# Transposing the normalised tiles of the first stage by DMA: 24 of 32 tiles leave TensorE, the projections keep two PSUM banks

## Chip, cores and metric

One Trainium2 chip, 8 NeuronCores, each running the same program on its own inputs with no traffic between cores. The metric is device time in microseconds (us) of the slowest core, median of several runs.

## The reference

For each of 4 sequences of 4096 tokens with 1024 features, a pre-norm attention and a pre-norm feed-forward layer, cut to what matters:

```python
z = layernorm(x)                            # no gain, no bias
q, k, v = z @ Wq, z @ Wk, z @ Wv            # 64 columns each
att = softmax(einsum('bid,bkd->bik', q, k), axis=1)   # over the queries i
x = x + tile(att @ v, (1, 1, 16))
z = layernorm(x); z_prev = z shifted by one token
r = sigmoid((mu_r*z + (1-mu_r)*z_prev) @ W_r.T)
k = (mu_k*z + (1-mu_k)*z_prev) @ W_k.T
x = x + r * (square(relu(k)) @ W_v.T)
```

The softmax runs over the queries, so every key row needs its exponentials over all 4096 queries before its sum is known. A core owns 2048 query tokens of one sequence, but computes q, k and v of all 4096.

## The kernel before, in words

**First stage.** x comes in 32 tiles of 128 tokens (128 x 1024, float32) into a ring of 8 buffers, `xst`. VectorE takes the statistics of each tile (`stats`: two halves and an aggregate, L405 to L408). GpSimd makes the scale from them (L352 to L357, two tiles at a time) and writes the normalised tile as bf16 into a ring of 8, `zst` (L363); its semaphore `G_Z` counts tiles, and SyncE waits for it before it reloads the buffer (`xst`, L307). TensorE transposes the tile in eight 128x128 pieces into PSUM (`T`, L704), and ScalarE (tiles 0 to 7) or VectorE (8 to 31) copies it to `zT` (L958, L416). `zT` holds two blocks of 8 tiles. Four tiles make a group n = 0 to 7: `QK(n)` projects q and k (L713), VectorE copies the result (`qk_evac`), `SW(n)` swaps the halves (L721, `sw_evac`), `MX(n)` computes scores of a sample of queries and `mx` the row maxima that the exponentials need. Every second group has `VP` and `VT` for v. All these share two PSUM banks, under the names `tb` and `tf`.

**Scores.** In between, TensorE computes scores in units of up to 128 keys x 1024 queries (`fill`, L759 and L763) into three PSUM tiles F0, F1, F2, and ScalarE exponentiates each (`exps`, L975). There are 136 units in eight groups; those of the last group, 72 from unit 64 on, need the maxima and copies of n = 7. The order is written out by hand for every engine; each engine runs its own list in order and waits on semaphores.

**Second stage.** When a key row kt has all its units, VectorE makes the scaled v (`vs`, L485) and TensorE adds its part of the output (`out_mm`, L771). From kt = 16 on VectorE also sums a reloaded tile of x behind it (`x_fold`, L475), which waits for that tile's DMA. `out_mm(kt)` of a later row waits for its `vs`. The exponentials of key rows from 20 on reuse a ring of four buffers (`Prot`) and wait for the `out_mm` of four rows earlier.

**Weights.** The three matrices of the feed-forward layer lie on the memory of `xst` and `zst`. GpSimd issues their loads (L372 to L376) when all tiles are normalised and transposed (`G_Z` and `P_T` at 32). The reloads of x into `x1` follow on SyncE (L316), one for each `out_mm` from the first on. In the last stage SyncE issues twelve DMA transposes of one 128x1024 bf16 tile each (L329).

Of the kernel before, what the change touches and what calls it, by code (L numbers as in the profile page):

```python
# [7 lines left out]
F32 = mybir.dt.float32  # L8
BF16 = mybir.dt.bfloat16
# [13 lines left out]
NA = 8  # L23
# [38 lines left out]
def build_program():  # L62
# [37 lines left out]

    ctx = ExitStack()
    e = ctx.enter_context
    with ctx:
# [11 lines left out]
        nmean = e(nc.sbuf_tensor("nmean", [128, TT], F32))  # L115
# [80 lines left out]
        F = [e(nc.psum_tensor(f"F{i}", [128, 1024], F32)) for i in range(3)]  # L196
# [13 lines left out]
        D_X = [sem(f"D_X{s}") for s in range(8)]  # L210
        D_R = [sem(f"D_R{t}") for t in range(TOWN)]
# [11 lines left out]
        V_T = sem("V_T")  # L223
# [48 lines left out]
        def wait_t(eng, i):  # L272
            if i < NA:
                eng.wait_ge(A_T, i + 1)
            else:
                eng.wait_ge(V_T, i - NA + 1)

        def t_bank(i):

            n, j = i // 4, i % 4  # L280
            if n == 0:
                return j % 2
            if j < 2:
                return n % 2
            return 1 if j == 2 or n % 2 == 0 else 0

# [16 lines left out]
        def _(sy):  # L303
            for i in range(TT):
                if i >= 8:
                    sy.wait_ge(G_Z, i - 7)
                sy.dma_start(out=xst[:, i % 8, :],  # L307
                             in_=x_in[i * 128:(i + 1) * 128, :]).then_inc(D_X[i % 8], 16)
                if i == 7:
                    sy.dma_start(out=identf[:, :], in_=idsw_in[:, 0:128]).then_inc(D_C, 16)  # L310
                    sy.dma_start(out=mu[:, :], in_=mu_in).then_inc(D_C, 16)
                    sy.dma_start(out=hmask[:, :], in_=hmask_in).then_inc(D_C, 16)
                    sy.dma_start(out=xh[:, :], in_=xh_in).then_inc(D_C, 16)
# [30 lines left out]
        def _(g):  # L344
            g.dma_start(out=idsw[:, :], in_=idsw_in).then_inc(D_ID, 16)
            g.dma_start(out=wqk[:, :, :].rearrange("p a b -> p (a b)"),
                        in_=wqk_in).then_inc(D_WQK, 16)
            g.wait_ge(V_C, 2)
            for h in range(TT // 2):
                a = 2 * h  # L350
                g.wait_ge(V_ST, 3 * (a + 2))
                g.tensor_scalar(nmean[:, a:a + 2], ag[:, a:a + 2, 0], -1.0, None,  # L352
                                ALU.mult).then_inc(G_ST, 1)
                g.tensor_scalar(vpe[:, a:a + 2], ag[:, a:a + 2, 1], EPS, None,
                                ALU.add).then_inc(G_ST, 1)
                g.wait_ge(G_ST, 3 * h + 2)
                g.tensor_tensor(rstd[:, a:a + 2], vpe[:, a:a + 2], mhalf[:, :],  # L357
                                ALU.pow).then_inc(G_ST, 1)
                g.wait_ge(G_ST, 3 * h + 3)
                for i in (a, a + 1):  # L360
                    if i >= 8:
                        g.wait_ge(P_T, i - 7)
                    g.tensor_scalar(zst[:, i % 8, :], xst[:, i % 8, :],  # L363
                                    nmean[:, i:i + 1], rstd[:, i:i + 1],
                                    ALU.add, ALU.mult).then_inc(G_Z, 1)
# [31 lines left out]
        def _(v):  # L397
# [3 lines left out]

            def stats(i):
                s = i % 4
                v.wait_ge(D_X[i % 8], 16 * (i // 8 + 1))
                v.bn_stats(bnst[:, s, 0:6], xst[:, i % 8, 0:512]).then_inc(V_ST, 1)  # L405
                v.bn_stats(bnst[:, s, 6:12], xst[:, i % 8, 512:1024]).then_inc(V_ST, 1)  # L406
                v.wait_ge(V_ST, 3 * i + 2)
                v.bn_aggr(ag[:, i, :], bnst[:, s, :]).then_inc(V_ST, 1)  # L408

            def t_evac(i):  # L410
                v.wait_ge(P_T, i + 1)
                sc = i // 8
                if i % 8 == 0 and sc >= 2:
                    v.wait_ge(P_QK, 2 * (sc - 2) + 2)
                    v.wait_ge(P_V, 2 * (sc - 2) + 2)
                v.tensor_copy(zT[:, sc % 2, :, (i % 8) * 128:(i % 8 + 1) * 128],  # L416
                              tb[t_bank(i)][:, :, :]).then_inc(V_T, 1)

            def qk_evac(n):
                v.wait_ge(P_QK, n + 1)  # L420
                v.tensor_copy(qk1[:, n * 512:(n + 1) * 512], tf[n % 2][:, :]).then_inc(V_QK, 1)

            def sw_evac(n):
                v.wait_ge(P_SW, n + 1)
# [12 lines left out]
            def mx(n):
                v.wait_ge(P_MX, n + 1)
                v.reduce_max(negm[:, 4 * n:4 * n + 4],
                             tf[n % 2][:, :].rearrange("p (a b) -> p a b", b=128),  # L440
                             axis=AX.X, negate=True).then_inc(V_MX, 1)

            def body(n):


                if 4 * n + 2 >= NA:
                    t_evac(4 * n + 2)
                    if n % 2 == 0:
                        vt_evac(n // 2 - 1)
                    t_evac(4 * n + 3)  # L450
                if n < 7:
                    stats(4 * n + 6)
                    stats(4 * n + 7)
                qk_evac(n)
                if n < 7 and 4 * n + 4 >= NA:
                    t_evac(4 * n + 4)
                sw_evac(n)
                if n < 7 and 4 * n + 5 >= NA:
                    t_evac(4 * n + 5)
                mx(n)  # L460
                if n % 2:
                    v_evac(n // 2)
                if n < 6:
                    stats(4 * n + 8)
                    stats(4 * n + 9)

            for i in range(6):
                stats(i)
            for n in range(8):
                body(n)  # L470
# [208 lines left out]
        def _(t):  # L679
# [3 lines left out]
            def T(i):  # L683
                j, n = i % 4, i // 4
                t.wait_ge(G_Z, i + 1)

                if j == 1 and n >= 1:
                    wait_t(t, i - 1)
                if j == 2:
                    if n == 0:  # L690
                        wait_t(t, i - 2)
                    elif n % 2 == 0:
                        t.wait_ge(V_MX, n)
                    else:
                        wait_t(t, i - 1)
                if j == 3:
                    if n == 0:
                        wait_t(t, i - 2)
                    elif n % 2 == 0:
                        wait_t(t, i - 1)  # L700
                    else:
                        t.wait_ge(V_MX, n)
                for ct in range(CT):
                    ins = t.transpose(tb[t_bank(i)][:, ct, :],  # L704
# [14 lines left out]
            def SW(n):  # L719
                t.wait_ge(V_QK, n + 1)  # L720
                t.matmul(tf[n % 2][:, :], swap, qk1[:, n * 512:(n + 1) * 512],  # L721
                         start=True, stop=True, skip_group_check=True).then_inc(P_SW, 1)

            def VP(sc):
                wait_t(t, min(8 * sc + 9, TT - 1))
                for ct in range(CT):
                    for h in range(2):
                        ins = t.matmul(tf[0][64 * h:64 * h + 64, :], wv[:, ct, :],  # L728
# [6 lines left out]
            def VT(sc):  # L735
                t.wait_ge(V_V, sc + 1)
                for m in range(4):
                    ins = t.transpose(tb[0][:, m, :],
                                      vT[:, sc % 2, m * 128:(m + 1) * 128], ident)
                ins.then_inc(P_VT, 1)  # L740

            def MX(n):
                t.wait_ge(V_SW, n + 1)
                for a in range(4):
                    kt = 4 * n + a
                    ins = t.matmul(tf[n % 2][:, a * 128:(a + 1) * 128],
                                   qk2[0:64, kt * 128:(kt + 1) * 128], qk1[0:64, 0:512:4],
                                   start=True, stop=True, skip_group_check=True,
                                   tile_position=(0, 0))
                ins.then_inc(P_MX, 1)  # L750

            def fill(u_):
# [3 lines left out]
                if u_ >= 3:  # L756
                    t.wait_ge(A_EXP, u_ - 2)
                f = F[u_ % 3]
# [18 lines left out]


            share = [0, 4, 8, 8, 10, 10, 10, 10]
            begun = 0  # L780

            def scores(n, p):
                nonlocal begun
                while begun < sum(share[:n]) + (p + 1) * share[n] // 8:
# [6 lines left out]
            for n in range(8):  # L791
                T(4 * n + 2)
                scores(n, 0)
                if n >= 2 and n % 2 == 0:
                    VT(n // 2 - 1)
                    scores(n, 1)
                T(4 * n + 3)
                scores(n, 2)
# [328 lines left out]
```

## Time and profile before

| | us |
|---|---|
| median of 3 runs (lowest to highest) | 414.08 (413.7 to 414.23) |
| the profiled execution, its own time | 413.11 |
| its span, first to last instruction, slowest core | 411.5 |
| spans of the 8 cores | 406.9 to 411.5 |

The profiled execution took 413.11 us, 1.6 us more than its span and 0.97 us less than the median. The page shows TensorE busy 79% of the span, VectorE 62%, ScalarE 56%, GpSimd 16%; these are means over stages that differ. The first stage ends at about 125 us, the exponentials at about 217 us, and the feed-forward layer fills the rest. A group of rows below is one view; a line of "..." stands for rows left out.

### The profile page before, as it was taken

The numbers are of one execution on the slowest core, as the hardware profiler recorded it, in microseconds if no ns is written. First come the engines' busy times: TensorE is split into PE (matmuls) and PEld (weight loads), VectorE is DVE, ScalarE is ACT, GpSimd is POOL, SyncE is SP. The second block draws the span as 40 slices with busy tenths as digits, with TensorE's granted clock in tenths as the row PEclk, the third lists the DMA queues.
The fourth block names the chain that finished last, engine by engine and source line by source line (L and its number), as shares of the span: only waits on it lengthen the run. The fifth ranks groups of instructions, "written<-read, shape, count | busy, mean of one in ns | idle before, by whom it ended". The sixth has DMA issues, their size and how long they took to land.

```text
span 411.5 us, 5646 instructions; the slowest of 8 cores (406.9 to 411.5 us)
## 1 busy us (share of the span) xinstructions
PE 323.8 (79%) x1683; PEld 136.3 (33%) x1706; DVE 254.6 (62%) x477; ACT 230.5 (56%) x358; POOL 65.2 (16%) x94
## 2 busy tenths in 40 slices
PE   0377679677795982787772599899999999999995
PEld 0233334233331220111111444344444444444442
DVE  3737777697721434754575998688748864773036
ACT  1233275399789996899994934900491048103510
POOL 1766345554510000000000002000100000000000
PEclk9996888699877796555555599999999999999998
DMA  7995455330069999950000000413131414130014
GB/s 178 312 310 172 109 200 204 103 104 2 0 109 159 156 190 273 346 202 2 0 1 0 2 1 13 91 53 154 27 65 50 168 25 76 53 144 12 0 46 160
DMA packets 23501, 43.90 MB, mean 107 GB/s; under 512 B 14256, under 2 KB 14640, under 8 KB 23088
## 3 DMA queue, kind: packets, MB, share of 16 engines
q1 hardware_dynamic: 22608, 36.78, 28.2%
q0 software_dynamic: 864, 6.75, 10.3%
q8 instruction: 15, 0.25, 0.3%
q14 instruction: 14, 0.11, 0.1%
HBM read 38.74 MB, written 8.39 MB: 115 GB/s over the span
## 4 chain that ended last, share of the span: by engine, by line
PE 54%; DVE 13%; ACT 12%; issue 9%; DMA 9%; POOL 1%; SPq 0%; DVEq 0%; ACTq 0%; POOLq 0%
PE F L905 13%; PE F L865 10%; PE F L883 10%; PE F L759 6%; DMA x<-x_in 6%; PE tf L713 5%; PE tb L704 4%; PE acc L771 3%; ACT Prot L975 3%; DMA xst<-x_in 3%; DVE bnst L405 2%; DVE zT L416 2%; ACT junk L975 2%; DVE bnst L406 2%; PE tf L728 2%
## 5 line engine op out<-in xcount | busy, mean ns | idle before, releaser
L759 PE MATMUL F<-qk 64*128 64x512 bf16 x136 | 64.3, 486 | 22.7 <-ACT Prot L975 6.8
L763 PE MATMUL F<-qk 64*128 64x512 bf16 x120 | 58.4, 501 | 0.0
L865 PE MATMUL F<-wr,xr 128*128 128x512 bf16 x251 | 57.3, 385 | 0.4 <-issue 0.2
L905 PE MATMUL F<-wv,ka 128*128 128x512 bf16 x252 | 55.7, 379 | 2.2 <-ACT ka L1034 1.8
L1026 ACT ACTIVATE rr<-F 128x1024 bf16<-128x1024 f32 x16 | 16.4, 1023 | 72.9 <-PE F L865 72.9
L883 PE MATMUL F<-dxk,wk 128*128 128x512 bf16 x249 | 55.5, 379 | 0.6 <-issue 0.2
L975 ACT ACTIVATE P<-F,negm 128x1024 bf16<-128x1024 f32 (+1 forms) x40 | 37.3, 948 | 28.8 <-PE F L759 23.3
L704 PE MATMUL tb<-idsw,zst 128*128 128x128 bf16 x256 | 23.4, 246 | 26.4 <-POOL zst L363 16.8
L975 ACT ACTIVATE junk<-F,negm 128x1024 bf16<-128x1024 f32 x32 | 37.1, 1174 | 5.5 <-PE F L763 5.4
L975 ACT ACTIVATE Prot<-F,negm 128x1024 bf16<-128x1024 f32 x32 | 36.7, 1198 | 5.4 <-PE F L763 5.4
L363 POOL TENSOR_SCALAR zst<-xst,nmean,rstd 128x1024 bf16<-128x1024 f32 x32 | 38.1, 1198 | 4.0 <-POOL rstd L357 3.7
L651 DVE TENSOR_TENSOR tmp<-F,rr 128x1024 f32<-128x1024 f32 x15 | 18.4, 1224 | 31.5 <-PE F L905 31.3
L759 PEld LDWEIGHTS F<-qk 64*128 64x128 bf16 x136 | 12.5, 97 | 75.2 <-issue 73.6
L975 ACT ACTIVATE junkL<-F,negm 128x1024 bf16<-128x1024 f32 x32 | 37.2, 1186 | 0.0
L865 PEld LDWEIGHTS F<-wr,xr 128*128 128x128 bf16 x256 | 25.5, 100 | 30.8 <-issue 1.9
L905 PEld LDWEIGHTS F<-wv,ka 128*128 128x128 bf16 x256 | 24.9, 98 | 32.1 <-issue 2.3
L883 PEld LDWEIGHTS F<-dxk,wk 128*128 128x128 bf16 x256 | 25.0, 98 | 30.6 <-issue 0.7
L475 DVE TENSOR_REDUCE xf<-x 128x64 f32<-128x1024 f32 x16 | 30.1, 1890 | 6.6 <-DMA x<-x_in 6.6
L713 PE MATMUL tf<-zT,wqk 128*128 128x512 bf16 x57 | 23.5, 582 | 9.7 <-ACT zT L958 3.6
L704 PEld LDWEIGHTS tb<-idsw,zst 128*128 128x128 bf16 x256 | 17.6, 109 | 35.6 <-issue 35.6
L556 DVE SCALAR_TENSOR_TENSOR xr<-dxk,mu,z1T 128x256 bf16<-128x256 bf16 (+1 forms) x72 | 27.2, 450 | 2.3 <-PE F L865 1.1
L405 DVE BATCH_NORM_STATS2 bnst<-xst 128x6 f32<-128x512 f32 x32 | 21.7, 678 | 7.8 <-DMA xst<-x_in 7.8
(102 smaller groups left out, 395.5 us busy)
## 6 DMA issues: line engine op xcount, KB each, us to landing
xst<-x_in SPq DMA_DIRECT2D x32, 512.0 KB, 5.3
x<-x_in SPq DMA_DIRECT2D x16, 512.0 KB, 23.9
y_out<-x SPq DMA_DIRECT2D x15, 512.0 KB, 2.6
wr<-wr_in POOLq DMA_DIRECT2D x1, 2048.0 KB, 17.9
wk<-wk_in POOLq DMA_DIRECT2D x1, 2048.0 KB, 30.9
wv<-wv_in POOLq DMA_DIRECT2D x1, 2048.0 KB, 44.9
y_out<-x SPq DMA_DIRECT2D x2, 256.0 KB, 2.0
wqk<-wqk_in POOLq DMA_DIRECT2D x1, 256.0 KB, 10.6
```

Of the source, the lines that this page charges most:

```text
L363: g.tensor_scalar(zst[:, i % 8, :], xst[:, i % 8, :], nmean[:, i:i + 1], rstd[:, i:i + 1], ALU.add, ALU.mult).then_inc(G_Z, 1)
L405: v.bn_stats(bnst[:, s, 0:6], xst[:, i % 8, 0:512]).then_inc(V_ST, 1)
L475: v.reduce_sum(xf[:, t_, :], x1[:, t_, :].rearrange("p (j d) -> p d j", d=D), axis=AX.X).then_inc(V_XF, 1)
L556: ins = v.scalar_tensor_tensor(xr[:, ct, o:o + w], dxk[:, q % 2, ct, o:o + w], mu[:, ct:ct + 1], z1T[:, ct, c0 - 1:c0 + w - 1], ALU.mult, ...
L704: ins = t.transpose(tb[t_bank(i)][:, ct, :], zst[:, i % 8, ct * 128:(ct + 1) * 128], ident)
L713: ins = t.matmul(tf[n % 2][:, :], wqk[:, ct, :], zT[:, (n // 2) % 2, ct, (n % 2) * 512:(n % 2 + 1) * 512], start=(ct == 0), stop=(ct == CT ...
L759: t.matmul(f[:, 0:512], qk2[0:64, kt * 128:(kt + 1) * 128], qk1[0:64, i0:i0 + 512], start=True, stop=True, skip_group_check=True, tile_pos ...
L763: t.matmul(f[:, 512:1024], qk1[64:128, kt * 128:(kt + 1) * 128], qk2[64:128, i0 + 512:i0 + 1024], start=True, stop=True, skip_group_check= ...
L865: ins = t.matmul(f[:, hh * 512:(hh + 1) * 512], xr[:, ct, j * 128:(j + 1) * 128], wr[:, ct, hh * 512:(hh + 1) * 512], start=(ct == 0), sto ...
L883: ins = t.matmul(F[k_ % 3][:, dd * 512:(dd + 1) * 512], wk[:, ct, dt * 128:(dt + 1) * 128], dxk[:, q % 2, ct, :], start=(ct == 0), stop=(c ...
L905: ins = t.matmul(F[(8 + j) % 3][:, hh * 512:(hh + 1) * 512], ka[:, dt, j * 128:(j + 1) * 128], wv2[:, dt, hh * 512:(hh + 1) * 512], start= ...
L975: sc.activation(dst, F[u_ % 3][:, 0:w], AF.Exp, bias=negm[:, kt:kt + 1], accum_out=ellp[:, ell_col[u_]:ell_col[u_] + 1]).then_inc(A_EXP, 1)
```

## The change

Tiles 0 to 7 are still transposed by TensorE and copied by ScalarE, but into two banks (`tx`) that lie under F2, which the score units leave alone until unit 20 (`NF2`); till then units alternate between F0 and F1. Tiles 8 to 31 are transposed by SyncE's DMA from `zst` to `zT`, and each transpose stands in SyncE's list ahead of a reload of `xst`. VectorE's 24 copies and TensorE's 192 transposing matmuls are gone. QK and MX now use the bank `tf[0]` alone, SW, VP and VT the other. GpSimd scales four tiles at a time from tile 8 on and takes the mean without negating it first. `wqk` is loaded once x tile 1 has landed. The lists of VectorE and TensorE are written out anew; 65 instead of 60 score units stand in the first stage.

```diff
@block.sync
-            for i in range(TT):
+            def load_x(i):
                 if i >= 8:
                     sy.wait_ge(G_Z, i - 7)
                 sy.dma_start(out=xst[:, i % 8, :],
                              in_=x_in[i * 128:(i + 1) * 128, :]).then_inc(D_X[i % 8], 16)
...
+            for i in range(TT):
+                if i >= NPT:
+                    sc = i // 8
+                    sy.wait_ge(G_Z, i + 1)
+                    if i % 8 == 0 and sc >= 2:
+                        sy.wait_ge(P_QK, 2 * (sc - 2) + 2)
+                        sy.wait_ge(P_V, 2 * (sc - 2) + 2)
+                    sy.dma_start_transpose(
+                        out=zT[:, sc % 2, :, (i % 8) * 128:(i % 8 + 1) * 128],
+                        in_=zst[:, i % 8, :]).then_inc(D_ZT[i % 8], 16)
+                if i + 8 < TT:
+                    load_x(i + 8)
@block.gpsimd
+            for n in range(2, 8):
+                scale(4 * n, 4, n + 2)
+                for i in range(4 * n, 4 * n + 4):
+                    apply(i)
 
             g.wait_ge(G_Z, TT)
-            g.wait_ge(P_T, TT)
+            for i in range(TT - 8, TT):
+                g.wait_ge(D_ZT[i % 8], 16 * (i // 8))
             g.dma_start(out=wr[:, :, :].rearrange("p a b -> p (a b)"),
                         in_=wr_in).then_inc(D_WR, 16)
@block.tensor
             def QK(n):
-                wait_t(t, 4 * n + 3)
-                if n >= 2 and n % 2 == 0:
-                    t.wait_ge(V_VT, n // 2)
+                if n == 0:
+                    t.wait_ge(D_WQK, 16)
+                if n < 2:
+                    t.wait_ge(A_T, 4 * n + 4)
+                else:
+                    for i in range(4 * n, 4 * n + 4):
+                        t.wait_ge(D_ZT[i % 8], 16 * (i // 8))
+                if n >= 1:
+                    t.wait_ge(V_MX, n)
                 for ct in range(CT):
-                    ins = t.matmul(tf[n % 2][:, :], wqk[:, ct, :],
+                    ins = t.matmul(tf[0][:, :], wqk[:, ct, :],
                                    zT[:, (n // 2) % 2, ct, (n % 2) * 512:(n % 2 + 1) * 512],
```

On SyncE's queue the 24 later loads of `xst` stood in one row of their own. Before:

```order
L307 DMA xst<-x_in 128x1024 x24
L316 DMA x<-x_in 128x1024 x16
```

Now a transpose goes ahead of each of the last 16, and eight transposes close the stage. Of the change, the queue from tile 8 on:

```order
L316 DMA_TRANSPOSE zT<-zst 128x8x128
L300 DMA xst<-x_in 128x1024
L316 DMA_TRANSPOSE zT<-zst 128x8x128
L300 DMA xst<-x_in 128x1024
L316 DMA_TRANSPOSE zT<-zst 128x8x128
```

So every load from tile 16 on has the transpose of the tile eight earlier ahead of it, and every transpose but the first has a load ahead of it.

On VectorE, around the evacuation of QK(3): tf0 and tf1 are the two banks, zT the copies of transposed tiles, and a pair of BN_STATS with its BN_AGGR is one tile's statistics. Before:

```order
L408 BN_AGGR ag<-bnst 128x2
L421 CAST qk1<-tf1 128x512
L416 COPY zT<-tb0 128x8x128
L425 CAST qk2<-tf1 128x512
L416 COPY zT<-tb0 128x8x128
L439 TENSOR_REDUCE negm<-tf1 128x4
L429 CAST vT<-tf0 128x512
L405 BN_STATS bnst<-xst 128x6
```

Of the change, from the statistics of tile 17 to the first half of tile 20's:

```order
L430 BN_AGGR ag<-bnst 128x2
L438 CAST qk1<-tf0 128x512
L425 BN_STATS bnst<-xst 128x6
L442 CAST qk2<-tf1 128x512
L456 TENSOR_REDUCE negm<-tf0 128x4
L428 BN_STATS bnst<-xst 128x6
L430 BN_AGGR ag<-bnst 128x2
L425 BN_STATS bnst<-xst 128x6
L428 BN_STATS bnst<-xst 128x6
L430 BN_AGGR ag<-bnst 128x2
L425 BN_STATS bnst<-xst 128x6
```

Before, the statistics of tiles 18 and 19 stood ahead of the CAST of QK(3), as the BN_AGGR above it shows; now they stand behind it, that is behind the transposes of tiles 12 to 15. The statistics of tiles 26 and 27 have moved behind the CAST of QK(5) in the same way.

## Rows read from the trace of the kernel before

**Rows 1.** The page: its first line and the DMA line of the 40 slices

```profile
span 411.5 us, 5646 instructions; the slowest of 8 cores (406.9 to 411.5 us)
...
DMA  7995455330069999950000000413131414130014
```

**Rows 2.** Busy time by stretch (PE, PEld, DVE, ACT, POOL, clock, DMA share, GB/s)

```profile
core 0: us, PE busy (x) PEld busy (x) DVE busy (x) ACT busy (x) POOL busy (x), PEclk, DMA share, GB/s
34.00:115.00 81.00, 62.26 (x413) 29.23 (x417) 60.38 (x113) 49.48 (x99) 42.06 (x59) 0.84 0.34 105
70.00:80.00 10.00, 6.42 (x36) 2.85 (x33) 7.87 (x16) 3.32 (x8) 3.53 (x5) 0.74 0.34 123
80.00:90.00 10.00, 7.56 (x60) 3.73 (x60) 8.02 (x15) 8.93 (x17) 4.72 (x9) 0.92 0.56 159
...
160.00:180.00 20.00, 12.85 (x50) 2.53 (x48) 13.37 (x21) 16.04 (x29) 0.00 (x0) 0.50 0.98 353
254.00:270.00 16.00, 14.10 (x65) 6.30 (x65) 11.62 (x27) 13.33 (x13) 1.02 (x2) 1.00 0.35 66
```

**Rows 3.** Timeline of GpSimd (start, length) at the weight loads

```profile
114.66 0.62 POOL L372 DMA_DIRECT2D wr<-wr_in  x1 [4.25 <-PE tb L704]
...
115.80 0.55 POOL L376 DMA_DIRECT2D wv<-wv_in  x1
```

**Rows 4.** The page's DMA issues: KB, us from issue to landing

```profile
wv<-wv_in POOLq DMA_DIRECT2D x1, 2048.0 KB, 44.9
```

**Rows 5.** Timeline of VectorE (idle before, and releaser, in brackets), 148 to 166 us

```profile
155.57 1.88 DVE L475 TENSOR_REDUCE xf<-x 128x64 f32<-128x1024 f32 x1 [3.02 <-DMA x<-x_in]
...
161.66 1.87 DVE L475 TENSOR_REDUCE xf<-x 128x64 f32<-128x1024 f32 x1 [3.54 <-DMA x<-x_in]
```

**Rows 6.** Timeline of ScalarE around the stop at 160 us

```profile
131.68 1.15 ACT L975 ACTIVATE junkL<-F,negm 128x1024 bf16<-128x1024 f32 x1
...
160.01 1.11 ACT L975 ACTIVATE Prot<-F,negm 128x1024 bf16<-128x1024 f32 x1 [1.75 <-PE F L763]
...
166.09 1.11 ACT L975 ACTIVATE junk<-F,negm 128x1024 bf16<-128x1024 f32 x1 [3.78 <-PE F L763]
```

**Rows 7.** SyncE's transposes of the last stage, L329: issue ns, and landing

```profile
L329 SPq DMA_TRANSPOSE z1T<-z x11: 1232/1232/1327, 255.3 to 344.6; - x11
...
DMA to landing us min/median/max: 3.0/3.1/4.7
```

**Rows 8.** SyncE's loads of x, L307: issue ns

```profile
L307 SPq DMA_DIRECT2D xst<-x_in x32: 327/328/886, 1.1 to 84.2; - x32
```

**Rows 9.** Timeline of VectorE in the first stage

```profile
29.23 0.69 DVE L439 TENSOR_REDUCE negm<-tf 128x4 f32<-128x512 f32 x1 [1.19 <-PE tf L746]
...
31.35 0.67 DVE L405 BATCH_NORM_STATS2 bnst<-xst 128x6 f32<-128x512 f32 x1
...
32.84 0.67 DVE L405 BATCH_NORM_STATS2 bnst<-xst 128x6 f32<-128x512 f32 x1
...
68.30 0.69 DVE L439 TENSOR_REDUCE negm<-tf 128x4 f32<-128x512 f32 x1
70.39 0.69 DVE L429 CAST vT<-tf 128x512 bf16<-128x512 f32 x1 [1.40 <-PE tf L728]
...
74.58 0.41 DVE L433 COPY v_sb<-tb 128x512 bf16<-128x512 bf16 x1
```

**Rows 10.** Timeline of GpSimd: one scaling and two applications, and a later power

```profile
33.40 0.22 POOL L354 TENSOR_SCALAR vpe<-ag 128x2 f32<-128x2 f32 x1
33.76 0.70 POOL L357 TENSOR_TENSOR rstd<-vpe,mhalf 128x2 f32<-128x2 f32 x1
34.71 2.38 POOL L363 TENSOR_SCALAR zst<-xst,nmean,rstd 128x1024 bf16<-128x1024 f32 x2 [0.24 <-POOL rstd L357]
...
251.05 2.45 POOL L384 TENSOR_TENSOR rstd<-vpe,mhalf 128x8 f32<-128x8 f32 x1 [134.70 <-DVE vpe L537]
```

**Rows 11.** Timeline of TensorE, a QK of tiles 12 to 15

```profile
61.87 2.99 PE L713 MATMUL tf<-zT,wqk 128*128 128x512 bf16 x7 [2.33 <-DVE zT L416]
```

More of the change, by code:

```diff
@@ L22 @@
 RC = 1.0 / C
-NA = 8
+NPT = 8
+NF2 = 20
 FBLK = [1, 2, 3, 0]
@@ L99, in build_program @@
             ps_after.append(cnt)
+    f_of = [u % 2 if u < NF2 else (u - NF2 + 2) % 3 for u in range(NU)]
+    f_prev = [max([p for p in range(u) if f_of[p] == f_of[u]], default=-1) for u in range(NU)]
     ctx = ExitStack()
@@ L193, in build_program @@
         w8 = tmp[:, 0:512].rearrange("p (a d) -> p a d", d=D)
-        F = [e(nc.psum_tensor(f"F{i}", [128, 1024], F32)) for i in range(3)]
+        F = [e(nc.psum_tensor(f"F{i}", [128, 1024], F32)) for i in range(2)]
+        tx_cm = [nc.psum_tensor(f"tx{i}", [128, 8, 128], BF16) for i in range(2)]
+        tx = opens(tx_cm)
+        closes(tx_cm)
+        F.append(e(nc.psum_tensor("F2", [128, 1024], F32)))
         tb_cm = [nc.psum_tensor(f"tb{i}", [128, 8, 128], BF16) for i in range(2)]
@@ L210, in build_program @@
         D_X = [sem(f"D_X{s}") for s in range(8)]
+        D_ZT = [sem(f"D_ZT{s}") for s in range(8)]
         D_R = [sem(f"D_R{t}") for t in range(TOWN)]
@@ L308, in _ @@
                              in_=x_in[i * 128:(i + 1) * 128, :]).then_inc(D_X[i % 8], 16)
[L309 to L313, printed above, removed]
+            for i in range(8):
+                load_x(i)
+            sy.dma_start(out=identf[:, :], in_=idsw_in[:, 0:128]).then_inc(D_C, 16)
+            sy.dma_start(out=mu[:, :], in_=mu_in).then_inc(D_C, 16)
+            sy.dma_start(out=hmask[:, :], in_=hmask_in).then_inc(D_C, 16)
+            sy.dma_start(out=xh[:, :], in_=xh_in).then_inc(D_C, 16)
+            for i in range(TT):
[10 more added lines that the diff above has]
+                    load_x(i + 8)
             for t_ in range(TOWN):
@@ L467, in _ @@
-            for i in range(6):
-                stats(i)
-            for n in range(8):
-                body(n)
+            for i in range(9):
+                stats(i)
+            qk_evac(0)
+            stats_a(9)
+            sw_evac(0)
+            stats_b(9)
+            mx(0)
+            for i in range(10, 14):
+                stats(i)
+            qk_evac(1)
+            stats_a(14)
+            sw_evac(1)
+            mx(1)
+            stats_b(14)
+            stats(15)
+            v_evac(0)
@@ new lines, in _ @@
+            vt_evac(0)
+            qk_evac(2)
+            stats_a(16)
+            sw_evac(2)
+            mx(2)
+            stats_b(16)
+            stats(17)
+            qk_evac(3)
+            stats_a(18)
+            sw_evac(3)
+            mx(3)
+            stats_b(18)
+            stats(19)
+            stats(20)
+            stats(21)
+            v_evac(1)
+            stats(22)
+            vt_evac(1)
+            stats(23)
+            qk_evac(4)
+            stats_a(24)
+            sw_evac(4)
@@ new lines, in _ @@
+            mx(4)
+            stats_b(24)
+            stats(25)
+            qk_evac(5)
+            stats_a(26)
+            sw_evac(5)
+            mx(5)
+            stats_b(26)
+            stats(27)
+            v_evac(2)
+            stats(28)
+            vt_evac(2)
+            stats(29)
+            stats(30)
+            stats(31)
+            qk_evac(6)
+            sw_evac(6)
+            mx(6)
+            qk_evac(7)
+            sw_evac(7)
+            mx(7)
+            v_evac(3)
@@ L737, in VT @@
                 for m in range(4):
-                    ins = t.transpose(tb[0][:, m, :],
+                    ins = t.transpose(tb[1][:, m, :],
                                       vT[:, sc % 2, m * 128:(m + 1) * 128], ident)
                 ins.then_inc(P_VT, 1)
[L742 to L750, printed above, removed]
             def fill(u_):
@@ L775, in out_mm, with scores @@
                              tile_position=(0, 64 * half)).then_inc(P_O, 1)
-            share = [0, 4, 8, 8, 10, 10, 10, 10]
             begun = 0
-            def scores(n, p):
+            def scores(n):
                 nonlocal begun
-                while begun < sum(share[:n]) + (p + 1) * share[n] // 8:
+                for _ in range(n):
                     fill(begun)
@@ L790, in _ @@
             T(1)
[L791 to L798, printed above, removed]
-                if n == 0:
-                    t.wait_ge(D_WQK, 16)
-                QK(n)
-                scores(n, 3)
-                if n < 7:
-                    T(4 * n + 4)
-                    scores(n, 4)
-                SW(n)
-                scores(n, 5)
-                if n < 7:
-                    T(4 * n + 5)
-                    scores(n, 6)
-                MX(n)
-                if n % 2:
-                    t.wait_ge(D_WV, 16)
-                    VP(n // 2)
-                scores(n, 7)
+            T(2)
+            T(3)
+            QK(0)
+            T(4)
+            T(5)
+            SW(0)
+            T(6)
+            MX(0)
+            scores(1)
+            T(7)
+            scores(1)
+            QK(1)
+            scores(2)
+            SW(1)
+            MX(1)
+            scores(1)
+            VP(0)
+            scores(2)
+            VT(0)
+            scores(3)
+            QK(2)
+            scores(2)
+            SW(2)
+            MX(2)
+            scores(6)
+            QK(3)
+            scores(2)
+            SW(3)
+            MX(3)
+            scores(1)
+            VP(1)
+            scores(3)
+            VT(1)
+            scores(7)
+            QK(4)
+            scores(3)
+            SW(4)
+            MX(4)
+            scores(4)
+            QK(5)
+            scores(3)
+            SW(5)
+            MX(5)
+            scores(1)
+            VP(2)
+            scores(3)
+            VT(2)
+            scores(8)
+            QK(6)
+            scores(3)
+            SW(6)
+            MX(6)
+            scores(3)
+            QK(7)
+            scores(3)
+            SW(7)
+            MX(7)
+            scores(1)
+            VP(3)
+            scores(2)
             VT(3)
```

166 lines of the change are left out of this document (67 added, 99 removed).

## Prediction

> **What bounds the kernel now.** I read the stretches first: from 34 to 115 us no engine is full; of 81 us TensorE is busy 62.3, VectorE 60.4, ScalarE 49.5, GpSimd 42.1, and the DMA engines 34% [rows 2]. The first stage is thus a loop of waits, tile by tile, and not a matter of one engine's work. Before 34 us the DMA slices show 9 and 9 [rows 1], the loads of x; the change leaves these tiles nearly as they are.
>
> What the stage's end releases is the next question. GpSimd issues the weight loads at 114.66 after 4.25 us of waiting for TensorE's last transposes [rows 3]. The third, issued at 115.80, lands 44.9 us later, at 160.7 [rows 3, 4]. The reloads of x share the DMA engines with them: VectorE gets the first at 155.57 and the second at 161.66, just behind the weights' end, after 3.02 and 3.54 us of waiting [rows 5]. Until that `x_fold` is done no later `vs` is, so `out_mm` and `Prot` stop: ScalarE stands 1.75 us to 160.01 and 3.78 us to 166.09 [rows 6]. From there it runs without a gap to the end of the stage, and the layer behind it follows. So the kernel's end hangs on the weight issue W = 114.66, one for one: what moves W moves the second reload, the restart at 166.09 and the end. ScalarE's own progress is the second string: it begins the last group at 131.68 [rows 6], and had 5.5 us of stops between that and 166.
>
> **The change part by part.** *Off TensorE, VectorE.* 192 small matmuls and 24 copies of some 0.7 us go; both engines had idle time, so I price that at what the waits below leave of it. *wqk later* stands behind the landing of tile 1; QK(0) waits for the copies of four tiles anyway; nothing, and if it came late it would cost QK(0) alone, with the loads of tiles 8 to 15 still hiding it. *F2 out of use until unit 20* costs ScalarE some alternation while it mostly waits for projections: nothing. *65 units instead of 60* fills ScalarE's gaps, off the path as long as W rules.
>
> *The DMA transposes* are the main term. In the last stage one takes 1.23 us of SyncE's issue and lands 3.1 us after its start [rows 7]. From 254 to 270 us four of them are the only traffic: 0.35 of 16 us, or 5.6 us of all 16 engines, 1.40 us each [rows 2]. So 1.23 us of issue, 1.40 us of transfer, 0.45 us to landing. The loads between them: 16 in 81 us at a share of 0.34 are 1.72 us each; 123 GB/s at 0.34 make 1.45 us for 524 KB, 159 GB/s at 0.56 make 1.85 [rows 2]. No trace of before has both kinds at once. The bounds for a pair of transpose and load, D: from below SyncE's issue of both, 1.23 + 0.33 = 1.56 us [rows 7, 8], if transfers overlap wholly; from above 1.40 + 1.85 = 3.25. One queue serves both in order, and each kind alone fills all engines, so I add: 1.40 + 1.55 (between 1.45 and 1.72) = **2.95 us**.
>
> A rule stands against that price. The Trainium skill, Advanced Engine Details and Errata, section X-Bar Transpose (TRN2), says transposing DMAs are as fast as ordinary ones; the measured figure of 261 GB/s in DMA: Bandwidth & Descriptors, section Latency and other measured facts, would give an estimated 1.00 us for 262 KB and D = 2.55. The trace's 1.40 us (187 GB/s) does not agree with either.
>
> *The chain to W.* All times are in the old clock, with these pieces: statistics of a tile 1.49 us, from 31.35 to 32.84 [rows 9]; evacuation of v 0.7 and 0.5 with its gap [rows 9]; application 1.19, a scale of four tiles 1.9 (0.36 to the power; the power 0.70 for 2 columns, 2.45 for 8, so 1.3 for 4; 0.25 behind it) [rows 10]; QK 3.1 from its inputs [rows 11]; from its end (64.86) to the end of `mx` 4.1 [rows 9, 11], less 0.3 for the copy no longer there, 3.8.
>
> 1. `mx(0)` ends at 29.9 [rows 9]; with half a statistics now ahead of it, 30.3. Tiles 10 and 11 follow to 33.3, scale and first application to 36.5, the issue to 37.8. There the transfer of tile 8's transpose starts; old load 16 was issued about then.
> 2. Tiles 8 to 15 follow without a pause, since GpSimd hands over a tile every 1.19 us and the queue wants D for it; tile 12 is normalised by 45.4, before its turn at 37.8 + 4D = 49.6. Tile 15 lands 7D + 1.40 + 0.45 later: 39.65 + 7D = 60.3. QK(3) starts there, about where it did (61.87) [rows 11].
> 3. But VectorE waits for QK(3) ahead of the statistics of tiles 18 and 19: 3.1 + 3.8, then 2.3 for the rest of tile 18 and tile 19: 9.2. GpSimd's 1.9 + 1.2 with 0.1 between, and the issue of 1.25: 4.45. DMA has nothing to do for all of it.
> 4. Tiles 16 to 23, eight pairs again: 7D + 1.85. QK(5) and the chain to tile 27: 9.2.
> 5. Tiles 28 to 31: statistics and two evacuations 7.2, scale 2.0, four applications 4.8, the last transpose 3.1: 17.1. There are no loads left, and four transposes keep up.
>
> W' = 39.65 + 7D + 9.2 + 4.45 + 7D + 1.85 + 9.2 + 17.1 = **81.45 + 14D**. At 2.95 it is 122.75, or 8.1 us later than 114.66. D = 2.37 breaks even.
>
> *Behind W.* VectorE's second reload comes 8.1 us later. ScalarE alone would begin the last group some 2 us later than 131.68: `mx(7)` at W' + 6.9 = 129.7, and units 62 and 63, now astride VP(3), cost 3.7 more: 133.4. Less than 8.1, so W rules, and the stop before 166 grows to about 12 us. TensorE's clock was 0.84 from 34 to 115 [rows 2]; QK(3) above ran at the lower level of 1.2 GHz by its 0.43 us a matmul, and I take that for all. The reduced work gives no reason for a better one.
>
> The profiled execution goes from 413.11 to 421.2; the median stands 0.97 us higher, so **422.2 us**.
>
> **Rivals.**
> - *The sum holds* (D 2.85 to 3.25): W' 121.35 to 126.95, 420.8 to 426.4 us. Chance 0.50.
> - *Partial overlap* of transfers, 2.45 to 2.85: 415.2 to 420.8. Speaks for it that a load's share may be waiting on memory that the other could use. 0.13.
> - *A transpose at the loads' rate*: half the bytes, half of 1.55 us, D = 2.33, W' 114.1: 413.5, no change. The last stage's 1.40 us speaks against it. 0.07. The skill's "as fast as regular DMAs" is this case.
> - *Faster: full overlap.* Under D = 2.2 or so the queue no longer binds; then four tiles land 4.7 + 3.1 = 7.8 us after their first is normalised. Tile 15 at 45.4 + 7.8 = 53.2; statistics to tile 19 at 62.4, to tile 23 at 69.6; 3.2 and 7.8 more put tile 23 at 80.6; + 9.2 + 17.1 = 106.9, W 7.8 us earlier, **406.3 us**. It decides at D = 2.37. For it: 66% of the DMA time is free from 34 to 115 us [rows 2]; against it: the transposes come in bursts, and in a burst the queue is what counts. 0.25, spread from 406.3 to 413.
> - *x comes without regard to W*: if the reloads passed the weights, ScalarE's string would rule, from 414.08 + 1.7 - 5.5 = 410.3 to 415.8. The second reload landing right behind the weights [rows 4, 5] speaks against it. 0.05, of it 0.04 faster.
>
> **How the numbers follow.** Some 0.2% (0.8 us) is what a measurement can tell from no change. Slower: 0.50 + 0.13 + 0.01 = 0.64; same 0.07; faster 0.25 + 0.04 = 0.29. The likeliest case alone has 420.8 to 426.4. The range must reach into the fast side till 2 in 10 are out: 408 to 427.
>
> **What would show it.** Transposes of tiles 9 to 15 and 17 to 23 landing some 3 us apart, each of the later ones over 6 us after its issue; DMA slices at 9 in two blocks, after 37 and after some 70 us, with a pause between; VectorE idle 5 us or more before the CASTs of QK(3) and QK(5); the weight issue near 123, the second reload near 170, ScalarE's stop before it about 12 us. Right for the rival: transposes 1.6 us apart and the issue before 114. Wrong both ways would be a weight issue that moves and an end that doesn't.

## The result, and the profile after

The changed kernel takes **476.38 us** (median of 4 runs, 476.13 to 477.45) against 414.15 beside it: ratio 1.151, 95% interval 1.148 to 1.153. It is 62 us slower; the prediction said 422.2 and a range from 408 to 427. In some executions of a kernel the cores of one die run at a lower granted clock and take longer; the medians and ratios here leave them out (the only one among these runs is an execution of e9_ahead_late_wv2 at 429.21 us). Below is the page of the changed kernel: its span, the busy times, two rows of the 40 slices, and the two groups that answer to the difference (count, busy us, mean ns | idle before and its releaser).

```profile
span 474.3 us, 5226 instructions; the slowest of 8 cores (469.8 to 474.3 us)
...
PE 317.2 (67%) x1514; PEld 124.9 (26%) x1514; DVE 238.5 (50%) x453; ACT 230.3 (49%) x358; POOL 140.5 (30%) x66
...
POOL 2998998099709971000000000020010000000000
...
DMA  8943499358912338999950000004222241322004
...
L374 POOL TENSOR_SCALAR zst<-xst,ag,rstd 128x1024 bf16<-128x1024 f32 x32 | 120.6, 3780 | 2.5 <-POOL rstd L364 2.5
...
L438 DVE CAST qk<-tf 128x512 bf16<-128x512 f32 x8 | 5.5, 692 | 96.3 <-PE tf L753 96.3
```

GpSimd was busy 65.2 us before (16% of the span) and is busy 140.5 us now. One group makes the difference: the normalisation, 32 times 3780 ns, where before two of them took 2.38 us [rows 10]. The kernel before adds the negated mean and multiplies; the changed one subtracts the mean and multiplies. VectorE has 96.3 us of idle time before the eight evacuations of QK. GpSimd's timeline of the changed kernel (start, length, in brackets idle time before):

```profile
11.03 7.55 POOL L374 TENSOR_SCALAR zst<-xst,ag,rstd 128x1024 bf16<-128x1024 f32 x2 [0.18 <-POOL rstd L364]
...
49.32 15.07 POOL L374 TENSOR_SCALAR zst<-xst,ag,rstd 128x1024 bf16<-128x1024 f32 x4 [0.24 <-POOL rstd L364]
...
94.44 0.23 POOL L361 TENSOR_SCALAR vpe<-ag 128x4 f32<-128x4 f32 x1 [13.00 <-DVE ag L430]
...
141.31 0.23 POOL L361 TENSOR_SCALAR vpe<-ag 128x4 f32<-128x4 f32 x1 [13.44 <-DVE ag L430]
...
159.66 15.07 POOL L374 TENSOR_SCALAR zst<-xst,ag,rstd 128x1024 bf16<-128x1024 f32 x4 [0.24 <-POOL rstd L364]
178.43 0.64 POOL L393 DMA_DIRECT2D wr<-wr_in  x1 [3.69 <-DMA zT<-zst]
```

The first two tiles take 7.55 us at 11.03, when no DMA transpose has been issued yet (the first is at 53.18). From tile 8 on four tiles take 15.07 us, so the transposes are handed to the queue one every 3.8 us. GpSimd still pauses twice, 13.00 and 13.44 us, for VectorE's statistics of tiles 19 and 27. The weights are issued at 178.43, 63.8 us later than at 114.66 [rows 3]. VectorE's two waits for reloads of x, as in [rows 5]:

```profile
212.13 1.88 DVE L525 TENSOR_REDUCE xf<-x 128x64 f32<-128x1024 f32 x1 [3.67 <-DMA x<-x_in]
...
224.49 1.86 DVE L525 TENSOR_REDUCE xf<-x 128x64 f32<-128x1024 f32 x1 [9.80 <-DMA x<-x_in]
```

The second comes at 224.49, 62.8 us later than before. So weight issue, second reload and end moved together, as the prediction had it (the third group of experiments tests the link itself), and what moved the weight issue by 63.8 in place of 8.1 us is to be found ahead of it.

### The profile page after: what moved, and what is told of

The parts are those of the page before. It is cut to its first block, busy times and chain, and to the rows that moved or that the text cites. A ratio compares the mean times of both kernels' runs of the same rounds, so it can differ in the third digit from the quotient of the medians.

```text
span 474.3 us, 5226 instructions; the slowest of 8 cores (469.8 to 474.3 us)
## 1 busy us (share of the span) xinstructions
PE 317.2 (67%) x1514; PEld 124.9 (26%) x1514; DVE 238.5 (50%) x453; ACT 230.3 (49%) x358; POOL 140.5 (30%) x66
## 4 chain that ended last, share of the span: by engine, by line
PE 39%; POOL 20%; issue 14%; DMA 10%; DVE 8%; ACT 7%; DVEq 0%; POOLq 0%; ACTq 0%; SPq 0%
POOL zst L374 17%; PE F L989 11%; PE F L949 9%; PE F L967 9%; DMA x<-x_in 7%; PE F L811 4%; PE acc L823 3%; PE tf L753 2%; DMA zT<-zst 2%; ACT Prot L1059 2%; POOL rstd L364 2%; DVE xr L606 2%; DMA xst<-x_in 1%; ACT z L1087 1%; ACT junkL L1059 1%
## 5 line engine op out<-in xcount | busy, mean ns | idle before, releaser
L374 POOL TENSOR_SCALAR zst<-xst,ag,rstd 128x1024 bf16<-128x1024 f32 x32 | 120.6, 3780 | 2.5 <-POOL rstd L364 2.5
L753 PE MATMUL tf<-zT,wqk 128*128 128x512 bf16 x64 | 28.6, 626 | 54.8 <-DMA zT<-zst 52.7
L438 DVE CAST qk<-tf 128x512 bf16<-128x512 f32 x8 | 5.5, 692 | 96.3 <-PE tf L753 96.3
L1059 ACT ACTIVATE junk<-F,negm 128x1024 bf16<-128x1024 f32 x32 | 37.5, 1185 | 32.8 <-PE F L815 32.8
L405 POOL TENSOR_TENSOR rstd<-vpe,mhalf 128x8 f32<-128x8 f32 (+1 forms) x2 | 3.3, 1646 | 139.9 <-DVE vpe L587 139.9
L1059 ACT ACTIVATE Prot<-F,negm 128x1024 bf16<-128x1024 f32 x32 | 36.6, 1198 | 2.6 <-PE F L815 2.6
L1059 ACT ACTIVATE junkL<-F,negm 128x1024 bf16<-128x1024 f32 x32 | 37.5, 1217 | 0.0
L738 PE MATMUL tx<-idsw,zst 128*128 128x128 bf16 x64 | 8.1, 307 | 32.7 <-POOL zst L374 32.7
```

Source lines behind the costliest of these rows:

```text
L374: g.tensor_scalar(zst[:, i % 8, :], xst[:, i % 8, :], ag[:, i, 0:1], rstd[:, i:i + 1], ALU.subtract, ALU.mult).then_inc(G_Z, 1)
L753: ins = t.matmul(tf[0][:, :], wqk[:, ct, :], zT[:, (n // 2) % 2, ct, (n % 2) * 512:(n % 2 + 1) * 512], start=(ct == 0), stop=(ct == CT - 1 ...
L1059: sc.activation(dst, F[f_of[u_]][:, 0:w], AF.Exp, bias=negm[:, kt:kt + 1], accum_out=ellp[:, ell_col[u_]:ell_col[u_] + 1]).then_inc(A_EXP, 1)
```

## Experiments

### First: the form of the normalisation

Two theories. **A**: GpSimd's new form, subtract and multiply with the mean read from `ag`, costs 3.78 us a tile; the rest of the change costs what the prediction's chain says. **B**: something else of the change (transposes on the same memory, the loop) slows GpSimd. The first run undoes the form alone in the changed kernel; the other three put it, or half of it, into the kernel before. The excerpts below show the normalisation alone; the tensor `nmean` and the negation that fills it come back in e1_add and go in e2_before_sub_ag.

```diff
 e1_add (the changed kernel)
...
-                                ag[:, i, 0:1], rstd[:, i:i + 1],
-                                ALU.subtract, ALU.mult)
+                                nmean[:, i:i + 1], rstd[:, i:i + 1],
+                                ALU.add, ALU.mult)
...
 e2_before_sub_ag (the kernel before)
...
-                                    nmean[:, i:i + 1], rstd[:, i:i + 1],
-                                    ALU.add, ALU.mult)
+                                    ag[:, i, 0:1], rstd[:, i:i + 1],
+                                    ALU.subtract, ALU.mult)
...
 e3_before_sub: ALU.subtract alone; nmean = 1.0 * mean
 e4_before_add_ag: ag[:, i, 0:1] alone, so the mean has the wrong sign
```

> The change with one part undone: GpSimd again negates the mean and applies it with add and multiply. Theory A (the form of the application is what costs): the application of a tile goes from 3.78 us back to 1.20, the weights are issued at 81.5 + 14 D us where D is the time of a transpose and a load on the queue, so 114 to 127 us for D of 2.4 to 3.25, and the time is 413 to 427 us. Rival B (the DMA transposes slow GpSimd or the loop as a whole): the application stays well over 1.20 us and the time stays above 450 us.

> The kernel before with that part alone: subtract and multiply, the mean read from ag, no negation. Theory A: 3.78 us a tile, GpSimd's 32 applications take 121 us in place of 38, the weight issue goes from 114.7 to some 150 to 160, the time to 450 to 460 us. Rival B: within 2 us of the kernel before, since nothing else of the change is there.

> The kernel before with subtract in place of add alone; the mean is copied to its own tensor without the sign. If the operation is what costs (A1): 3.78 us a tile and the time of the run before this one. If the operand read from ag is (A2): 1.20 us and about 414 us.

> The kernel before with add, but the mean read from ag, whose sign is the other one: the normalised tiles are then x plus the mean, the amount of work is the same. A1 (the operation): 1.20 us a tile, about 414 us. A2 (the operand, one column of pairs): 3.78 us and 450 to 460 us.

Measured: e1_add 426.03 us, ratio 1.028 (1.027 to 1.030); e2_before_sub_ag 453.36, ratio 1.094 (1.092 to 1.096); e3_before_sub 461.05 and e4_before_add_ag 414.88 (one run each), with 414.27 for the kernel before beside all four. The normalisation's group on the pages of e2_before_sub_ag, e3_before_sub and e4_before_add_ag, in this order:

```profile
L361 POOL TENSOR_SCALAR zst<-xst,ag,rstd 128x1024 bf16<-128x1024 f32 x32 | 120.9, 3785 | 3.6 <-POOL rstd L355 2.2
```

```profile
L363 POOL TENSOR_SCALAR zst<-xst,nmean,rstd 128x1024 bf16<-128x1024 f32 x32 | 121.0, 3784 | 4.0 <-POOL rstd L357 4.0
```

```profile
L363 POOL TENSOR_SCALAR zst<-xst,ag,rstd 128x1024 bf16<-128x1024 f32 x32 | 38.0, 1193 | 4.0 <-POOL rstd L357 3.3
```

The operand from `ag` costs nothing (1193 ns, against 1198 in the kernel before); subtraction costs 2.59 us a tile. B is out as the cause of the slow normalisation: the kernel before, without one DMA transpose in that stage, has the same 3.78 us. Two more runs asked whether it is the place of the subtraction in the pair.

```diff
 e10_mult_sub; e11_mult_add has ALU.add there (nmean holds mean * rstd)
...
-                                    nmean[:, i:i + 1], rstd[:, i:i + 1],
-                                    ALU.add, ALU.mult)
+                                    rstd[:, i:i + 1], nmean[:, i:i + 1],
+                                    ALU.mult, ALU.subtract)
```

> The kernel before, with the application written as x times rstd, less mean times rstd; the product is made beside the scale. It asks whether the slow thing is subtraction in the first place of the pair or anywhere. If anywhere: 3.78 us a tile, about 455 to 461 us. If only in the first place: 1.20 us and about 415 us.

> The same with add in the second place, so the mean's product is added with the wrong sign and the tiles hold other values; the work is that of the run before. If the order of the two operations costs nothing: 1.20 us a tile and 414 to 416 us. If a multiplication ahead is itself slow: 3.78 us and about 455 us, and the run before says nothing on subtraction.

Measured: 458.16 and 413.25 us, one run each. The one run of the kernel before beside them took 417.92, some 4 us more than its other runs, so the reading goes by the group of each:

```profile
L364 POOL TENSOR_SCALAR zst<-xst,rstd,nmean 128x1024 bf16<-128x1024 f32 x32 | 120.9, 3785 | 3.6 <-POOL nmean L358 3.4
```

```profile
L364 POOL TENSOR_SCALAR zst<-xst,rstd,nmean 128x1024 bf16<-128x1024 f32 x32 | 37.9, 1190 | 3.6 <-POOL nmean L358 2.9
```

Subtraction is slow in either place, and multiplication in the first place is not. Why GpSimd's subtraction is slower than its addition no run shows.

### Second: what the rest of the change costs, and where

With the addition restored the changed kernel issues its weights at 128.73; the prediction's chain gave 122.75. Below are GpSimd's and SyncE's timelines of e1_add (SPq is the time in which SyncE issues; the transposes are those of tiles 8, 14, 15, 16 and 23), and the landing of the transpose issued at 55.23:

```profile
70.66 0.23 POOL L362 TENSOR_SCALAR nmean<-ag 128x4 f32<-128x4 f32 x1 [22.81 <-DVE ag L433]
...
110.15 0.23 POOL L362 TENSOR_SCALAR nmean<-ag 128x4 f32<-128x4 f32 x1 [25.91 <-DVE ag L433]
...
119.00 4.72 POOL L377 TENSOR_SCALAR zst<-xst,nmean,rstd 128x1024 bf16<-128x1024 f32 x4 [0.24 <-POOL rstd L367]
128.73 0.62 POOL L396 DMA_DIRECT2D wr<-wr_in  x1 [5.00 <-DMA zT<-zst]
```

```profile
35.22 1.33 SPq L317 DMA_TRANSPOSE zT<-zst  x1
...
51.32 3.21 SPq L317 DMA_TRANSPOSE zT<-zst  x1
...
55.23 1.76 SPq L317 DMA_TRANSPOSE zT<-zst  x1
...
74.00 1.22 SPq L317 DMA_TRANSPOSE zT<-zst  x1
...
94.14 1.92 SPq L317 DMA_TRANSPOSE zT<-zst  x1
```

```profile
DMA to landing us min/median/max: 6.2/6.2/6.2
```

GpSimd now pauses 22.81 and 25.91 us for VectorE's statistics, and normalises its last four tiles in 4.72 us. Tile 8's transfer starts at the end of its issue, 36.5; tile 15's lands at 55.23 + 6.2 = 61.4. Less the 1.85 us of the last transpose, over seven pairs: 3.29 us a pair. The second block, from 75.2 to 94.14 + 6.3, gives 3.34. With these, 81.45 + 7 x (3.29 + 3.34) = 127.9, against 128.73. This is core 1, the slowest. The same count on the other seven cores of the trace gives 2.88 to 3.26 us in the first block and 2.86 to 3.23 in the second, with weight issues from 122.9 to 128.5. The busy times of e1_add in the two blocks and the two pauses:

```profile
core 1: us, PE busy (x) PEld busy (x) DVE busy (x) ACT busy (x) POOL busy (x), PEclk, DMA share, GB/s
36.50:61.50 25.00, 15.19 (x58) 4.68 (x58) 9.69 (x19) 12.57 (x28) 8.40 (x9) 0.66 1.17 242
61.50:75.00 13.50, 8.80 (x47) 3.12 (x47) 9.07 (x18) 5.20 (x12) 3.87 (x6) 0.86 0.05 19
75.20:100.50 25.30, 9.26 (x37) 2.70 (x35) 6.76 (x15) 15.16 (x27) 8.36 (x9) 0.64 1.16 239
100.50:114.00 13.50, 10.80 (x53) 3.69 (x53) 8.58 (x18) 9.23 (x19) 3.38 (x5) 0.75 0.05 20
```

In a block the queue is full; between the blocks the DMA share is 5%. A share over 1 counts packets of one engine that are open at the same time twice, so it gives no price; the landings do. On the slowest core a pair costs 3.29 and 3.34 us, 0.2 more than the 1.40 + 1.72 of the two kinds apart and just above the prediction's upper bound of 3.25; on most other cores it lies within the 2.85 to 3.25 of *The sum holds*. The slowest core sets the time. Now VectorE in e1_add, from the statistics of tile 17 past the evacuation of QK(3) to tile 19's:

```profile
56.77 0.67 DVE L428 BATCH_NORM_STATS2 bnst<-xst 128x6 f32<-128x512 f32 x1
...
65.38 0.69 DVE L441 CAST qk<-tf 128x512 bf16<-128x512 f32 x1 [7.04 <-PE tf L756]
...
68.92 0.67 DVE L428 BATCH_NORM_STATS2 bnst<-xst 128x6 f32<-128x512 f32 x1
```

VectorE is idle for 7.04 us behind tile 17, for a QK that waits for transposes, while tiles 18 and 19 wait for their statistics. Two kernels test the two parts: one moves the statistics ahead in VectorE's list, the other halves the loads of tiles 16 to 31 to see what a load is worth in a pair.

```diff
 e5_stats_ahead (e1_add, VectorE's list)
             vt_evac(0)
+            stats(16)
+            stats(17)
+            stats(18)
+            stats(19)
             qk_evac(2)
-            stats_a(16)
+            stats_a(20)
...
 e7_half_loads (e1_add)
...
+                w = C if i < 16 else C // 2
-                sy.dma_start(out=xst[:, i % 8, :],
-                             in_=x_in[i * 128:(i + 1) * 128, :]).then_inc(D_X[i % 8], 16)
+                sy.dma_start(out=xst[:, i % 8, 0:w],
+                             in_=x_in[i * 128:(i + 1) * 128, 0:w]).then_inc(D_X[i % 8], 16)
```

> The run with the addition restored, and VectorE's list changed alone: the statistics of tiles 16 to 19 stand ahead of the evacuation of QK(2), those to 22 ahead of QK(3), to 26 ahead of QK(4), to 30 ahead of QK(5). Theory A (two pauses of the DMA queue, 61.5 to 75 and 100.5 to 114 us, come from statistics that wait behind a QK): the queue runs through sixteen pairs from 36.5 us at 3.35 us each, to 90; the weights are issued near 102 us, 26 us earlier than in that run and 13 us earlier than before the change, and the time is 399 to 404 us. Rival B (something else in the loop, TensorE's order or the two PSUM banks, holds the tiles back as soon as the statistics don't): the pauses shrink by less than half, the weight issue stays over 115 us and the time over 412 us.

> The run with the addition restored, with the loads of x tiles 16 to 31 cut to the first 512 of 1024 columns; the other columns are those of an older tile, so these tiles' values are others, and the work behind is the same. It measures what of the 3.35 us of a pair is the load. Theory A (the queue adds the two up): a pair takes 3.35 less 0.8 to 0.9, 2.5 us, the chain gives a weight issue at 81.5 + 14 x 2.5 = 116.5 us, and the time is about 414 us. Rival B (a transpose among loads costs 3 us by itself, the load is hidden): a pair stays over 3.1 us, the issue over 125 us, the time over 422 us.

Measured: e5_stats_ahead **403.17 us**, ratio to the kernel before 0.974 (0.973 to 0.976); e7_half_loads 418.76 (one run); the kernel before beside both took 414.01. Of e5_stats_ahead: VectorE at tiles 17 and 18, at QK(2) and at QK(4); GpSimd's pause before tiles 24 to 27, its last normalisation and the weight issue; and the busy times from 34 to 100 us:

```profile
46.74 0.69 DVE L428 BATCH_NORM_STATS2 bnst<-xst 128x6 f32<-128x512 f32 x1 [1.48 <-DMA xst<-x_in]
...
49.34 0.69 DVE L428 BATCH_NORM_STATS2 bnst<-xst 128x6 f32<-128x512 f32 x1 [1.01 <-DMA xst<-x_in]
...
53.77 0.69 DVE L441 CAST qk<-tf 128x512 bf16<-128x512 f32 x1
...
80.26 0.69 DVE L441 CAST qk<-tf 128x512 bf16<-128x512 f32 x1 [4.93 <-PE tf L755]
```

```profile
85.00 0.23 POOL L362 TENSOR_SCALAR nmean<-ag 128x4 f32<-128x4 f32 x1 [10.15 <-DVE ag L433]
...
95.72 4.72 POOL L377 TENSOR_SCALAR zst<-xst,nmean,rstd 128x1024 bf16<-128x1024 f32 x4 [0.24 <-POOL rstd L367]
104.72 0.62 POOL L396 DMA_DIRECT2D wr<-wr_in  x1 [4.28 <-DMA zT<-zst]
```

```profile
34.00:100.00 66.00, 44.49 (x200) 14.31 (x198) 40.41 (x80) 44.41 (x89) 36.13 (x40) 0.78 0.97 214
```

At tiles 17 and 18 VectorE now waits for loads, and QK(2) is ready when it gets there. The weights go at 104.72 (expected near 102), 24.0 us earlier than in e1_add, and the time falls by 22.9. A holds, B doesn't. But the queue does not run full to the end, as A expected: the mean share of 0.97 is made of 1.20 from 37.5 to 72 us, 1.02 to 85.7 and 0.59 from there to 100. The statistics of tile 27 still stand behind QK(4), for which VectorE waits 4.93 us, and GpSimd waits 10.15 us for them; so this order is not the best one. By the count used above the first seven pairs cost 3.11 us each here, and the first eleven 2.95: what a pair costs is no constant. Of e7_half_loads, the transposes of tiles 8 and 15, the landing of the latter, and the weight issue:

```profile
34.47 1.33 SPq L318 DMA_TRANSPOSE zT<-zst  x1
...
52.18 1.22 SPq L318 DMA_TRANSPOSE zT<-zst  x1
```

```profile
DMA to landing us min/median/max: 5.5/5.5/5.5
```

```profile
120.30 0.62 POOL L397 DMA_DIRECT2D wr<-wr_in  x1 [5.79 <-DMA zT<-zst]
```

(52.18 + 5.5 - 1.85 - 35.8) / 7 = 2.86 us a pair in the first block, 2.63 by the same count in the second; the chain gives 119.9, the trace 120.30. Halving the load took 0.4 to 0.7 us off a pair, not the 0.8 to 0.9 that A expected, so the time missed 414 by 5. B, which had a pair stay over 3.1 us, doesn't hold either: on the other cores of this trace a pair costs 2.35 to 2.86 us. So the load is part of the price, but halving it saves less than half of the 1.45 to 1.72 us of a load alone; whether the rest lies with the transpose or with the halved rows stays open.

### Third: the link from the weights to the end

Two theories on how the weight issue moves the end. **A**: the reloads of x share the DMA engines with the weights and so land late, and VectorE and ScalarE wait for the second one. **B**: ScalarE's own progress rules, and the reloads only seem to bind. If A holds, putting the third weight load behind the last reload must free ScalarE's two stops.

```diff
 e8_before_late_wv2 (the kernel before), e9_ahead_late_wv2 (e5_stats_ahead)
...
+            g.wait_ge(D_R[TOWN - 1], 16)
             g.dma_start(out=wv2[:, :, :].rearrange("p a b -> p (a b)"),
```

> The kernel before, with the third weight load issued only once the last reload of x has landed; nothing else. Theory A (the end hangs on the weight issue because the second reload of x lands behind the weights): the reloads then run at full rate from the end of the second weight load at about 146 us, VectorE has both before it asks for them at 152.5 and 158, ScalarE's two stops of 5.5 us before 166 us go, and the time is 408 to 410 us. Rival B (the link is ScalarE's own progress, the reloads only seem to bind): within 1.5 us of the kernel before. If the third load were then late for its matmuls at 267 us, the time would rise instead; it lands about 190.

> The run with addition restored and statistics ahead, plus the same wait. There the stops before 156 us were 1.4 and 5.1 us. Theory A: both go, 396 to 398 us. Rival B: 402 to 404 us.

Measured: e8_before_late_wv2 408.05 us, ratio 0.986 (0.985 to 0.987); e9_ahead_late_wv2 **397.4 us**, ratio 0.960 (0.958 to 0.961). GpSimd's and ScalarE's timelines of e8_before_late_wv2, and GpSimd's of e9_ahead_late_wv2; of ScalarE's rows these are all with idle time before them between 115 and 214 us:

```profile
115.56 0.62 POOL L372 DMA_DIRECT2D wr<-wr_in  x1 [4.28 <-PE tb L705]
...
171.04 0.53 POOL L377 DMA_DIRECT2D wv<-wv_in  x1 [54.32 <-DMA x<-x_in]
```

```profile
120.38 1.11 ACT L976 ACTIVATE junk<-F,negm 128x1024 bf16<-128x1024 f32 x1 [1.61 <-PE F L760]
...
213.88 0.60 ACT L988 ACTIVATE tmp<-acc 128x512 f32<-128x512 f32 x1 [2.18 <-PE acc L772]
```

```profile
105.20 0.62 POOL L396 DMA_DIRECT2D wr<-wr_in  x1 [4.31 <-DMA zT<-zst]
...
160.55 0.53 POOL L401 DMA_DIRECT2D wv<-wv_in  x1 [54.19 <-DMA x<-x_in]
```

The third load goes 54 us later, at 171.04; the reloads of x land 11 to 17 us after their issue, where it was 17 to 28 in the kernel before; and ScalarE has no stop left between 120.4 and 213.9. The 5.7 and 5.8 us gained compare with stops of 5.5 us in the kernel before [rows 6] and 1.4 + 5.1 us in e5_stats_ahead. A holds in both. The table puts the weight issue W of each profiled execution beside its median, both less those of the kernel before (114.66; 414.0 to 414.3). Taken alone it would not tell A from B, since ScalarE's last group also waits for the end of the first stage:

| kernel | W | its shift | shift of the time |
|---|---|---|---|
| after | 178.43 | +63.8 | +62.2 |
| e3_before_sub | 161.55 | +46.9 | +46.8 |
| e10_mult_sub | 159.5 | +44.8 | +44.0 |
| e2_before_sub_ag | 154.69 | +40.0 | +39.1 |
| e1_add | 128.73 | +14.1 | +11.8 |
| e7_half_loads | 120.30 | +5.6 | +4.7 |
| e4_before_add_ag | 115.8 | +1.1 | +0.6 |
| e11_mult_add | 115.1 | +0.4 | -0.9 |
| e5_stats_ahead | 104.72 | -9.9 | -10.8 |

e8_before_late_wv2, which changes nothing ahead of W, has it at 115.56: from one execution to another W moves by about 1 us by itself. For e10_mult_sub and e11_mult_add the 414.15 of the result stands in for the kernel before.

## Why the prediction was wrong, step by step

- **"Application 1.19"** in the chain to W is the step that failed. The prediction took it from the add and multiply of the kernel before and carried it over to subtract and multiply, another operation for which no row stood; it gave this term neither a bound nor a rival. It measured 3.78 us. Undoing it gives back 50.4 of the 62.2 us (476.38 to 426.03). The 2.59 us a tile come to 82.9 us over 32 tiles; W took 49.7 of them; GpSimd's two pauses for statistics, 22.81 and 25.91 us in e1_add, shrank to 13.00 and 13.44 and so hid most of the rest.
- **D = 2.95 us**: one queue that binds in a burst was right, and the size was 0.36 too small on the slowest core: 3.29 and 3.34. By 14 D this is 5 us of the 6.0 that e1_add's W is over the 122.75 of the prediction. On the other cores of e1_add D was 2.86 to 3.26, and 2.95 over the first eleven pairs of e5_stats_ahead. So the rivals "partial overlap" (under 2.85), "at the loads' rate" and "full overlap" are out for these bursts. That the price of a pair is that of a load plus that of a transpose was not borne out to the letter, as the halved loads show. The 261 GB/s of the Trainium skill (DMA: Bandwidth & Descriptors, section Latency and other measured facts) would give an estimated 1.00 us a transpose. The traces don't agree: it takes 1.40 us alone, and a pair costs no less than load and transpose apart on the slowest core.
- **The constants, 81.45 us**: with the measured D, e1_add's W comes out within 0.9 us and that of e7_half_loads within 0.4. In part this is luck. In e1_add the first transfer starts 1.25 us earlier than the chain's 37.8, the pause between the blocks is 13.8 us where the chain has 13.65, and the way from the end of the second block to W takes 28.3 us where it has 26.3; and W scatters by about 1 us. The pauses behind QK(3) and QK(5) are where the prediction put them; e5_stats_ahead shows that the order of VectorE's list makes them, since they shrink with all transposes kept.
- **W and the end one for one**: right within 2.3 us over shifts from -10 to +64 (table), and by its cause (third group). That e1_add's 426.03 us falls within the 420.8 to 426.4 of the likeliest case is partly luck again: its W is 6.0 us over the prediction's, and its end comes 2.3 us sooner behind W than one for one.
- **Priced at nothing**: the later `wqk`, F2's absence until unit 20, 65 units, the two PSUM banks. In e1_add chain and trace differ by 0.9 us before W, a sum of errors of both signs, so each of these may have cost or gained 1 or 2 us. None was tried alone.
- **The predicted signs**: in the changed kernel itself the places are right and the times are not (weight issue 178, not 123; second reload 224, not 170), and its transposes come 3.8 us apart, too far to fill the queue. e1_add shows the signs: W 128.73, two full blocks, a pause behind each.

So the change had three parts that oppose each other: subtraction, 50 us lost; the order of VectorE's list, 23 us lost; and the DMA transposes, which with addition and a better order are 10.8 us ahead of the kernel before. Whether the kernel before would gain from another order by itself was not tried, so the 10.8 us belong to the two together.

## What to carry to other kernels

A changed operation code is a changed instruction: price it from its own row, and where none is there, say that the price is unknown and leave room for a multiple, above all on GpSimd. When a transfer joins an in-order queue, ask first which engine's list will wait for it and what stands behind that wait; moving that work ahead gave back 22.9 us here. And a stage's end that releases a long transfer may reach the kernel's end only through what that transfer delays; the part of it that isn't needed soon can be issued last.

## What the runs showed of the hardware

- GpSimd's TENSOR_SCALAR on 128x1024 (float32 in, bf16 out, two scalars per partition) takes 1.19 to 1.20 us with add and mult in either order (kernel before, e4_before_add_ag, e11_mult_add) and 3.78 to 3.79 us with subtract in either place (changed kernel, e2_before_sub_ag, e3_before_sub, e10_mult_sub): 3.2 times.
- A 128x1024 bf16 DMA transpose mostly lands 3.0 to 3.1 us after its issue when alone [rows 7], and 4.9 to 8.4 us after it within e1_add's bursts with 512 KB loads (all but the first of each burst). A pair then takes 3.3 us on the slowest core and 2.9 to 3.3 on the others, and SyncE's issue of a transpose stretches from 1.22 to as much as 3.21 us (tile 14 above).
- A 512 KB reload of x landed 17 to 28 us after its issue beside the weight loads of the kernel before, and 11 to 17 us with the third weight load held back (e8_before_late_wv2).
- GpSimd's power on 128x4 took 1.03 us, where 1.3 was estimated from 2 and 8 columns.
